# Stage boundaries of a four-stage attention and feed-forward program: who clears semaphores, who normalises, where waits stand

## The reference

```python
mod = (silu(c) @ wmod).reshape(8, 6, 1, 256)            # sa, ca, ga, sb, cb, gb
h = layernorm(x) * (1 + ca) + sa
x = x + ga * causal_attention(h)                        # 16 heads of 16 channels
h = layernorm(x) * (1 + cb) + sb
x = x + gb * ffn(h)
# ffn: two layers, each
#   t = shift_token(x); q, k, v = split(t @ wqkv)       # 8 heads of 64
#   q, k = rotary_xpos(l2norm(q) * qs, l2norm(k) * ks)  # tables cos*scale, sin*scale, ...
#   x = x + local_attention(q, k, v) @ wo               # windows of 128, with the one before
#   t = layernorm(shift_token(x)) * g + b
#   x = x + (a * gelu(gate)) @ w2 + b2,  a, gate = split(t @ w1 + b1)
```

## Time and profile before

| what | value |
|---|---|
| median of 3 runs | 5578.67 us (5578.08 to 5596.92) |
| profiled execution: time, span | 5582.27 us, 5580.5 us |
| TensorE busy | 79% of the span |
| VectorE busy | 59% |
| ScalarE busy | 47% |
| GpSimd busy | 34% |
| mean granted clock of TensorE | 0.876 |

### The profile page before, as it was taken

One profiled execution on the slowest core, in us unless ns is written; L12 is line 12 of the kernel. 1 busy time (PEld: TensorE's weight loads), 2 busy tenths in 40 slices (PEclk: granted clock), 3 DMA queues, 4 the chain that ended last, 5 costly groups with the idle time before them and its releaser, 6 DMA issues. The chain is left out here.

```text
span 5580.5 us, 99747 instructions
## 1 busy us (share of the span) xinstructions
PE 4388.4 (79%) x33294; PEld 3169.1 (57%) x33294; DVE 3284.6 (59%) x7520; ACT 2599.3 (47%) x5522; POOL 1905.4 (34%) x1485
## 2 busy tenths in 40 slices
PE   2888888888883878878778888758878788787886
PEld 1444444444443666666666666646666666666665
DVE  2665566556553755756657566555657556575564
ACT  0344444444453544545445454444545445454453
POOL 3122231221323433434334333334434344343443
PEclk6788888899896999989899899879899999999988
DMA  4324424333412000000000000010000000000000
GB/s 102 82 38 93 101 66 71 94 88 51 93 39 62 11 15 14 11 15 11 13 16 11 13 13 11 15 56 17 16 20 16 19 17 19 20 14 20 17 19 18
DMA packets 155749, 200.46 MB, mean 36 GB/s; under 512 B 29900, under 2 KB 130728, under 8 KB 155184
## 3 DMA queue, kind: packets, MB, share of 16 engines
q1 hardware_dynamic: 151088, 192.13, 14.3%
q10 hardware_dynamic: 4096, 1.06, 0.1%
HBM read 116.02 MB, written 67.68 MB: 33 GB/s over the span
## 5 line engine op out<-in xcount | busy, mean ns | idle before, releaser
L1487 POOL TENSOR_TENSOR b_e<-b_e,b_share 128x512 f32<-128x512 f32 (+1 forms) x512 | 533.9, 1043 | 1283.2 <-DVE b_share L1915 1283.2
L968 DVE TENSOR_REDUCE a_mx<-a_ring 128x2 f32<-128x1024 f32 (+3 forms) x768 | 724.6, 955 | 327.9 <-PE a_ring L789 203.9
L637 ACT ACTIVATE a_e_t<-a_ring 128x1024 f32<-128x1024 f32 (+3 forms) x768 | 603.6, 809 | 621.1 <-PE a_ring L789 392.8
L1590 ACT ACTIVATE b_e<-b_e,b_bias 128x256 f32<-128x256 f32 (+1 forms) x1024 | 498.7, 488 | 616.1 <-DVE b_bias L1895 614.8
L1693 PE MATMUL b_bank_m<-b_h_t_hi,b_w_hi 128*128 128x256 f32 x1584 | 475.5, 300 | 99.7 <-POOL b_h_t_lo L1493 76.2
L1693 PE MATMUL b_bank_p<-b_wqkv_hi,b_turned_hi 128*128 128x512 f32 x768 | 369.5, 481 | 184.2 <-ACT b_qk L1562 140.6
L802 PE MATMUL a_ring<-a_k_st,a_q_st 48*128 48x512 f32 (+3 forms) x1536 | 361.7, 469 | 146.3 <-ACT a_e_t L637 94.1
L1693 PE MATMUL b_bank_m<-b_h_t_lo,b_w_hi 128*128 128x256 f32 x1584 | 460.9, 291 | 0.0
L1693 PE MATMUL b_bank_m<-b_h_t_hi,b_w_lo 128*128 128x256 f32 x1584 | 459.8, 290 | 0.0
L827 PE MATMUL a_ring<-a_q_st,a_k_st 50*128 50x512 f32 (+3 forms) x1536 | 362.6, 471 | 108.6 <-DVE a_qk_p L947 64.2
L1895 DVE CUSTOM_DVE_ANT_0 b_e<-b_bank_s,b_mask,b_scale_q 128x256 f32<-128x256 f32 (+1 forms) x1024 | 433.5, 459 | 0.7
(11 more groups left out here) (220 smaller groups left out, 11074.1 us busy)
## 6 DMA issues: line engine op xcount, KB each, us to landing
a_q_st<-a_parts_q SPq DMA_DIRECT2D x192, 128.0 KB, 4.4
a_k_st<-a_parts_k SPq DMA_DIRECT2D x192, 128.0 KB, 7.4
b_fl<-f_rows SPq DMA_DIRECT2D x72, 256.0 KB, 4.0
a_parts_q<-a_qk_p SPq DMA_DIRECT2D x16, 1024.0 KB, 9.4
a_parts_k<-a_qk_p SPq DMA_DIRECT2D x16, 1024.0 KB, 4.0
a_xl<-in_L_attn_x SPq DMA_DIRECT2D x9, 1024.0 KB, 9.2
f_rows<-b_fr SPq DMA_DIRECT2D x33, 256.0 KB, 2.3
b_x_l<-x_rows SPq DMA_DIRECT2D x33, 256.0 KB, 3.7
```

The source lines that it names most:

```text
L637: act.activation(e_t[:, step % 2, 2 * pair:2 * pair + 2, 0:cols], slot[:, :].rearrange("p (h t) -> p h t", h=2)[:, :, 0:cols], ACT.Exp).th ...
L968: dve.reduce_max(mx[:, g % 2, :, pair, piece, t:t + 1], slot[:, :].rearrange("p (r c) -> p r c", r=2)[:, :, 0:cols], AX.X)\
L1487: pool.tensor_tensor(weights, weights, share[:, pp, :].unsqueeze(2) .broadcast_to([P, 2, 2 * WIN - lo]), ALU.mult).then_inc(e_done.sem, 1)
L1590: ins = act.activation(weights, weights, ACT.Exp, scale=-1.0, bias=bias[:, pp, hh:hh + 1], accum_out=total[:, pp, hh:hh + 1])
```

## The change

- `clear` and `prime` deal their semaphores out to the five engines, each taking every fifth.
- Attention, lead: VectorE takes the statistics of sample 0 before `w_lo`, and itself normalises and modulates `xl`; its wait for the constants moves behind the projections. `x_statistics(1)` and `nearer("x", 1)` move into the row of 24 reductions, behind the 13th and the 19th. ScalarE's wait for `lo_split` moves down. SP issues `load_x(1, 1)` right behind stacks 0, and stacks 1 ahead of stacks 2.
- Attention, closing: VectorE adds the second half of x1, takes all statistics together, normalises all 8 tiles of `f_t`, and modulates 6 of them; GpSimd modulates the last 2.
- Layers: the first half of `fl` and the scales are loaded first; the tables are stored on the host so that a partition's 8 rows are adjacent (2 KB); the second half of `fl` comes behind the tables. Tables and scales count on a semaphore of their own (`tab_loaded`). The waits for weights, tables and vectors move from ahead of the body into the steps that use them (and are then executed for every sample).

```diff
 def clear(nc, sems):
     with nc.Block() as block:
+        @block.sync
+        def _(sp):
+            for s in sems[0::NENG]:
+                sp.sem_clear(s)
+
         @block.gpsimd
         def _(pool):
-            for s in sems:
+            for s in sems[1::NENG]:
                 pool.sem_clear(s)
...
 def prime(nc, signals):
...
+        @block.vector
+        def _(dve):
+            for s in signals[4::NENG]:
+                dve.sem_inc(s.sem, s.at(0, 0))
...
-            for half in range(CK):
-                store_parts(2 * half, 0)
-                store_parts(2 * half + 1, 0)
-                load_stacks(2 * half, 0)
+            store_parts(0, 0)
+            store_parts(1, 0)
+            load_stacks(0, 0)
             load_x(1, 1)
+            store_parts(2, 0)
+            store_parts(3, 0)
             load_stacks(1, 0)
+            load_stacks(2, 0)
             load_stacks(LAST, 0)
...
-            modulate_x(0)
+            pool.sem_inc(x_scaled.sem, 2)
+            pool.sem_inc(x_scaling.sem, 1)
             modulate_x(1)
...
+                if closing:
+                    rows, shape = f_t[:, END:TB, :], [P, TB - END, C]
+                    pool.wait_ge(end_scaled, 1)
+                    pool.tensor_tensor(rows, rows, modb[:, 2:3, :].broadcast_to(shape), ALU.mult)\
+                        .then_inc(end_scaled, 1)
+                    pool.wait_ge(end_scaled, 2)
+                    pool.tensor_tensor(rows, rows, modb[:, 1:2, :].broadcast_to(shape), ALU.add).then_inc(end_done, 1)
...
-            dve.wait_ge(const_made, 16)
...
                 if mode == "lead":
                     x_statistics(0)
+                    dve.wait_ge(hi_split, 3)
+                    dve.tensor_tensor(w_lo[:, :, :, :], w_raw, w_hi[:, :, :, :].bitcast(F32), ALU.subtract)\
+                        .then_inc(lo_split, 1)
                     nearer("x", 0)
+                    dve.wait_ge(rstd_of["x"].sem, rstd_of["x"].at(0, 1))
+                    step(normalise(xl, xl, "x", range(TB)))
+                    dve.wait_ge(mod_in_loaded.sem, mod_in_loaded.at(0, 1))
+                    step(dve.tensor_tensor(xl[:, :, :], xl[:, :, :], mod_in[:, 1:2, :].broadcast_to([P, TB, C]),
+                                           ALU.mult))
+                    dve.tensor_tensor(xl[:, :, :], xl[:, :, :], mod_in[:, 0:1, :].broadcast_to([P, TB, C]),
+                                      ALU.add).then_inc(h_ready.sem, 1)
...
-                    x_statistics(1)
-                    nearer("x", 1)
                     for k in range(NUNIT):
                         reduce_unit(0, k, 0)
+                        if k == NUNIT // 2:
+                            x_statistics(1)
+                        if k == NUNIT * 3 // 4:
+                            nearer("x", 1)
...
-            for u in range(NU):
+            for u in range(NU // 2):
                 sp.dma_start(fl[:, blocks_of(u), :], rows_of(f_in, 0, u)).then_inc(f_loaded[u // 2].sem, 16)
-
+            sp.dma_start(qk_scale[:, 0, :], qs.partition_broadcast(P)).then_inc(tab_loaded, 16)
+            sp.dma_start(qk_scale[:, 1, :], ks.partition_broadcast(P)).then_inc(tab_loaded, 16)
...
-                sp.dma_start(tab[:, n // 2, n % 2, :, :], tables[n].rearrange("(w p) d -> p w d", p=P))\
-                  .then_inc(small_loaded, 16)
+                sp.dma_start(tab[:, n // 2, n % 2, :, :], tables[n].rearrange("(p w) d -> p w d", p=P))\
+                  .then_inc(tab_loaded, 16)
+            for u in range(NU // 2, NU):
+                sp.dma_start(fl[:, blocks_of(u), :], rows_of(f_in, 0, u)).then_inc(f_loaded[u // 2].sem, 16)
...
-            pe.wait_ge(lo_split, len(pieces))
...
+                        if u < 0 and m == 0:
+                            pe.wait_ge(lo_split, len(pieces))
...
+                        if pp == FIRST:
+                            pe.wait_ge(lo_split, CK)
...
-            dve.wait_ge(small_loaded, 16 * NSMALL)
-            dve.wait_ge(tab_made, 4)
-            dve.wait_ge(const_made, n_const)
+            dve.wait_ge(const_made, n_const - 1)
...
+                        if pp == FIRST:
+                            dve.wait_ge(const_made, n_const)
+                            dve.wait_ge(tab_made, 4)
+                            dve.wait_ge(small_loaded, 16 * NSMALL)
```

More of the change, by code:

```diff
@@ L40, with _ @@
 VW = 32
+NENG = 5
 def clear(nc, sems):
     with nc.Block() as block:
+        @block.sync
+        def _(sp):
+            for s in sems[0::NENG]:
+                sp.sem_clear(s)
         @block.gpsimd
         def _(pool):
-            for s in sems:
+            for s in sems[1::NENG]:
                 pool.sem_clear(s)
+        @block.scalar
+        def _(act):
+            for s in sems[2::NENG]:
+                act.sem_clear(s)
+        @block.tensor
+        def _(pe):
+            for s in sems[3::NENG]:
+                pe.sem_clear(s)
+        @block.vector
+        def _(dve):
+            for s in sems[4::NENG]:
+                dve.sem_clear(s)
 class Semaphores:
@@ L64, in prime, with _ @@
     with nc.Block() as block:
+        @block.sync
+        def _(sp):
+            for s in signals[0::NENG]:
+                sp.sem_inc(s.sem, s.at(0, 0))
         @block.gpsimd
         def _(pool):
-            for s in signals:
+            for s in signals[1::NENG]:
                 pool.sem_inc(s.sem, s.at(0, 0))
+        @block.scalar
+        def _(act):
+            for s in signals[2::NENG]:
+                act.sem_inc(s.sem, s.at(0, 0))
+        @block.tensor
+        def _(pe):
+            for s in signals[3::NENG]:
+                pe.sem_inc(s.sem, s.at(0, 0))
+        @block.vector
+        def _(dve):
+            for s in signals[4::NENG]:
+                dve.sem_inc(s.sem, s.at(0, 0))
 class Signal:
@@ L359, in attention_stage @@
         lo_split = plain("a_w_lo_split")
+        end_scaled = plain("a_end_scaled")
+        end_done = plain("a_end_done")
+        END = 6
         x_loaded = sig("a_x_loaded", 1, 16)
@@ L577, in body @@
                 pool.wait_ge(biased.sem, biased.at(i, 1))
-                for p in range(2):
+                for p in range(1 if closing else 2):
                     pool.wait_ge(gated.sem, gated.at(i, 2 * p + 2))
@@ L932, in nearer, with normalise @@
                         .then_inc(rstd_of[name].sem, 1)
+                def normalise(dst, src, name, ts):
+                    n = norms[name]
+                    for t in ts:
+                        ins = dve.tensor_scalar(dst[:, t, :], src[:, t, :], n["aggr"][:, t, 0:1], n["rstd"][:, t:t + 1],
+                                                ALU.subtract, ALU.mult)
+                    return ins
                 def low(what, done, a):
@@ L1146, in rotary_tables @@
     cos, sin, scale = two(np.cos(freqs), np.cos(freqs)), two(-np.sin(freqs), np.sin(freqs)), two(scale, scale)
-    return np.stack([cos * scale, sin * scale, cos / scale, sin / scale]).astype(f)
+    rows = np.stack([cos * scale, sin * scale, cos / scale, sin / scale]).astype(f)
+    return np.ascontiguousarray(rows.reshape(4, NWIN, P, D2).transpose(0, 2, 1, 3)).reshape(4, T, D2)
 def plan_mlp():
```

43 lines of the change are left out of this document (29 added, 14 removed).

## The result

The changed kernel takes 5496.78 us in the median of 4 runs (5493.1 to 5505.67), the kernel before, on the same chip, 5579.47 (5578.08 to 5596.92). The ratio is 0.985 with a 95% interval of 0.9829 to 0.9871: 82.7 us less by the medians, where 95.2 were forecast. The profiled execution took 5493.1 with a span of 5491.3, 89.2 less than the span before. The time of 5496.78 lies in the range given, 13 above the forecast.

The account below looks back on a forecast made before the run. Stage boundaries, where a loss holds up all engines, were taken as the bound the change touches: 21.7 + 20.0 + 21.5 + 10.9 + 23.6 - 2.5 = 95.2 us less, median 5483.5, range 5466 to 5506.

Parts of the forecast that it names:

- Clearing and priming: Stage boundaries and the end: semaphores dealt to five engines, the slowest deciding, win 21.7 us (bounds 16 to 24).
- The normalised input: Attention lead: sample 0's modulated input ready at 55.8 instead of 75.76, 20.0 us earlier (bounds 18 to 21).
- bounds 18 to 21: GpSimd's masks: Attention lead: bounds on the 20.0 us, given because GpSimd makes masks until 51.8 beside VectorE's normalisation.
- The first pass: Attention lead: reductions start at about 109.75, maxima come at 134.9 instead of 156.44, 21.5 us won.
- The closing: End of attention: VectorE takes over most of GpSimd's work, ending at 1717.8, 10.9 us won (bounds 9.5 to 12.2).
- Layer starts: Start of both layers: weights and tables land sooner, 11.8 us each, 23.6 in all (bounds 4 to 12.5 each).
- The loops: Layer loops: moved waits, run for every sample, lose 0.15 x 16 = 2.5 us (bounds 0 to 10).
- the rival on the clock in the loops: Loops: less rest at boundaries lowers TensorE's granted clock; 4.2 us more per sample cancels the gain; chance 0.02.
- The layers' loads: Layer starts, rival: tables or vectors land as late as now, a layer wins 4, not 11.8: 5499; chance 0.13.
- bound by transfers: Attention lead, rival: x shares engines with stacks 0, or stacks 1 make TensorE wait, 6 us later: 5490; chance 0.11.
- The clock did not come back sooner: Attention lead, rival: without idle time TensorE may keep 2.4 GHz, 8 us more won: 5475; chance 0.11.

Follow-up runs that it names:

- p_sems: Only the dealing of semaphore clears and primes to five engines, on the kernel before: 5559.83 us, ratio 0.9961.
- the repeat: The changed kernel run again unaltered: 5504.62 us, ratio 0.9862 to the kernel before.
- p_closing: Only the attention closing changed, on the kernel before: 5576.11 us, ratio 0.9992.

## Why the prediction was right

**Clearing and priming.** Forecast 21.7, measured 20.1 by the four stretches in the changed kernel as in p_sems. The mechanism held; mis-sized was TensorE's pitch, taken as GpSimd's plus 34 ns (0.105 and 0.117) and measured at 0.127 and 0.150.

**The normalised input.** Forecast 20.0, measured (75.76 - 30.94) - (51.87 - 26.23) = 19.2. The eight tensor_scalar were put at 3.1, from the 128-column row and the slope of two-input ones. Alone they take 2.7; here they took 4.30, since a fill of `k_st` ran until 43.35 and the masks until 47.07. Two errors of opposite sign, and the step "bounds 18 to 21: GpSimd's masks" held the answer without the mechanism.

**The first pass.** Forecast 21.5; measured 40.3 - 19.2 = 21.1. The time was right and the attribution was not: x's place in SP's queue carries it.

**The closing.** Forecast 10.9, measured 10.5, again by errors that cancel. I set 1.2 aside for the two products beside GpSimd; they took 1.76 each, as without it, because GpSimd was done at 1667.57. The 2.0 lost were in the tensor_scalar (4.63 against 2.68). The rule was known, its field was not: I applied it to operations with two inputs, put the condition that GpSimd reads on the 2-port mode as well, and overlooked that it names tensor_scalar.

**Layer starts.** Forecast 23.6, measured 22.7 in the first profile, 20.3 in the repeat, 19.5 alone. The projection at 20.95 was forecast at 20.6; the tables at 18.2, and they came at 19.1 to 21.2. The reason given, that they need more than the 215 GB/s of 256-byte rows, was wrong: with such rows the product still starts at 21.3 and 21.4, most likely since GpSimd no longer waits for the vectors behind them.

**The loops.** I took off 2.5 for the moved waits. They cost under 0.9 a layer, most likely nothing. The profile was 6.0 short of the forecast: 4.1 outside the loops, and 1.9 because the loops grew by 4.4 and not by 2.5. That growth lies within the scatter of the loops: over the 14 profiles the attention loop came out at 1523.4 to 1564.2, with TensorE's granted clock, layer 0 at 1820.7 to 1833.7, layer 1 at 1851.4 to 1862.6, with the granted clock only in part. That the forecast of the loops came within 2 us is luck. By the ratios the gain is 84 and, in the repeat, 77, where the stretches outside the loops give 93.6 and 90.3. The loops with the change may so be some 10 longer on the average. The profiles say less: the three loops together take 5216.5 to 5228.2 in the five profiles with one part of the change or none, 5223.3 on the average, and 5215.1 to 5243.0 in the nine others, 5230.0 on the average. Whether less rest at the boundaries lowers the granted clock (the rival on the clock in the loops, at a small fraction of its price) or the runs just fell so is open.

**The other rivals.** The layers' loads came sooner, as forecast. The lead was not bound by transfers: between its first reduction (86.46) and 124.70 VectorE waits neither for x nor for stacks. TensorE's first scores still wait for stacks 0, 3.41 us against 2.67 before. The clock did not come back sooner: from 86.46 to 111.41 it is granted at 0.52, and from there to 135.00 at 0.50.

## What to carry to other kernels

Cut every profile at the same few places and compare stretch by stretch: edits of 2 to 40 us are then plain, while the time of one and the same kernel moves by 15 from run to run (5493.1 to 5508.6). Before work is given to VectorE, look at what GpSimd runs at that moment, fills included, and at whether the new instruction is a tensor_scalar; help from GpSimd can cost more than it carries. And when a transfer and its consumer are moved together, test each alone: in the lead the place in the queue did it. Where a load is moved and given a semaphore of its own in one edit, look at which transfer released its consumer before.

## What the chip showed that was not expected

- A tensor_scalar of VectorE with 128x8 elements lasted 4.51 to 4.58 us, until a GpSimd fill of 32x8192 ended; one of 256 columns costs 0.33 alone and 0.51 to 0.58 beside GpSimd's masks and products.
- Two Newton instructions on two columns took 1.19 and 1.20 beside GpSimd products of 1.24 each, 0.16 alone.
- A satisfied wait on VectorE costs some 0.05 us where nothing covers it; a semaphore clear 0.073 on GpSimd and 0.127 on TensorE.
- The same loop of 11,712 matmuls took between 1523.4 and 1564.2 us, at granted clocks of 0.89 and 0.85.
- A sample of layer 0 took 228.5 to 228.9 us in the profile of the kernel before and 227.9 to 231.9 in that of p_closing, whose layer stages are the same.
